# A two-layer decoder on one core: the large buffer moved to a multiple of 512 bytes, and expert blocks loaded plainly and turned on TensorE

## The reference, cut to what matters

```python
x = x + L0_attn(layernorm(x))          # windowed attention
x = x + L0_xattn(ctx, layernorm(x))    # 8 heads of 128 over 1536 keys (context and x)
x = x + L0_ffn(layernorm(x))           # ternary weights, depthwise convolution
x = x + L1_attn(layernorm(x))          # 16 heads of 16
x = x + L1_xattn(layernorm(x), ctx)
x = x + L1_ffn(layernorm(x))           # each token goes to one of 8 experts:
#   idx = argmax(softmax(x @ Wg + bg));  y = gelu(x @ W1[idx] + b1[idx]) @ W2[idx] + b2[idx]
```

## Time and profile before

| | us |
|---|---|
| median of 3 runs | 2080.79 (2079.79 to 2083.28) |
| the profiled execution | 2085.14 |
| its span, first to last instruction | 2083.3 |
| latent stages of the four batches, about | 60 to 285, 560 to 770, 1040 to 1260, 1530 to 1760 |
| first load of a new block leaves | 2025.98 |
| last scatter starts | 2078.86 |

### The profile page before, as it was taken

How to read it: one execution, slowest core, us unless ns; L and a number is a source line. 1 busy time by engine, 2 the same in 40 slices (tenths; PEclk the granted TensorE clock), 3 DMA queues, 4 the chain that set the end, 5 groups by cost and what they waited for, 6 DMA issues and landing times.

```text
span 2083.3 us, 41861 instructions
## 1 busy us (share of the span) xinstructions
PE 1849.1 (89%) x17118; PEld 1032.0 (50%) x17118; DVE 1634.8 (78%) x2654; ACT 1281.7 (62%) x1921; POOL 213.8 (10%) x223
## 2 busy tenths in 40 slices
PE   4999988989899987889899998898989998898967
PEld 2666653323566663232457665242356666333235
DVE  7888878697788877689688887969687887869944
ACT  5666646568566645749656664657756664574932
POOL 1000001110100001030100000120010000103513
PEclk8999999999999999999999999999999999999988
DMA  7477730000277760001157673001127666001125
GB/s 303 88 124 122 123 81 12 9 27 22 59 129 123 122 125 18 6 23 33 31 103 125 122 124 64 13 9 27 42 57 120 123 122 127 8 6 48 58 78 114
DMA packets 450766, 159.93 MB, mean 77 GB/s; under 512 B 426213, under 2 KB 441840, under 8 KB 450064
## 3 DMA queue, kind: packets, MB, share of 16 engines
q1 hardware_dynamic: 448192, 150.89, 35.9%
q0 software_dynamic: 2384, 6.36, 0.9%
HBM read 33.96 MB, written 9.47 MB: 21 GB/s over the span
## 4 chain that ended last, share of the span: by engine, by line
PE 49%; DVE 29%; DMA 9%; ACT 6%; issue 4%; SPq 1%; POOL 1%; POOLq 0%; DVEq 0%; ACTq 0%
DVE nmx L2234 15%; DMA arena<-arena 8%; PE ps L772 8%; PE ps L774 7%; PE ps L773 7%; PE ps L1154 6%; PE ps L944 3%; PE ps L1140 3%; DVE arena L2044 3%; PE ps L938 2%; PE ps L939 2%; PE ps L1104 1%; PE ps L1164 1%; DVE st L1866 1%; ACT arena L1542 1%
## 5 line engine op out<-in xcount | busy, mean ns | idle before, releaser
L2234 DVE TENSOR_REDUCE nmx<-ps 128x2 f32<-128x1024 f32 x384 | 444.4, 1217 | 14.0 <-PE ps L1104 12.5
L1714 ACT ACTIVATE arena<-ps 128x512 f32<-128x512 f32 x768 | 406.4, 600 | 47.8 <-PE ps L1140 43.4
L2029 DVE TENSOR_SCALAR_CACHE_REDUCE ps<-ps 128x1536 f32<-128x1536 f32 x128 | 225.7, 1763 | 44.2 <-PE ps L774 43.6
L1154 PE MATMUL ps<-arena 128*17 128x256 f32 x3072 | 240.0, 389 | 0.0
L2044 DVE SCALAR_TENSOR_TENSOR arena<-arena,rs 128x1536 f16<-128x1536 f32 x128 | 231.6, 1809 | 4.2 <-ACT arena L1604 4.2
L1604 ACT ACTIVATE arena<-arena,rs 128x1536 f16<-128x1536 f32 x128 | 200.8, 1569 | 42.9 <-DVE rs L2035 42.9
L1595 ACT ACTIVATE arena<-ps,nm 128x1536 f32<-128x1536 f32 x128 | 197.1, 1540 | 13.5 <-DVE ps L2029 13.5
L772 PE MATMUL ps<-arena 128*128 128x512 f16 (+2 forms) x508 | 176.4, 349 | 13.9 <-issue 7.0
L938 PE MATMUL ps<-arena 128*128 128x128 f16 x1536 | 185.3, 219 | 1.1 <-DMA arena<-arena 1.0
L939 PE MATMUL ps<-arena 128*128 128x128 f16 x1536 | 185.2, 219 | 0.0
L774 PE MATMUL ps<-arena 128*128 128x512 f16 (+2 forms) x508 | 176.2, 349 | 0.0
(11 more groups left out here) (350 smaller groups left out, 3562.5 us busy)
## 6 DMA issues: line engine op xcount, KB each, us to landing
arena<-in_weights SPq DMA_DIRECT2D x8, 929.0 KB, 21.1
arena<-arena SPq DMA_DIRECT2D x72, 64.0 KB, 2.1
arena<-arena SPq DMA_TRANSPOSE x268, 3.7
arena<-in_ctx SPq DMA_DIRECT2D x4, 1024.0 KB, 5.4
arena<-in_ctx_t SPq DMA_DIRECT2D x4, 1024.0 KB, 5.0
arena<-in_experts SPq DMA_DIRECT2D x1, 3840.0 KB, 11.7
arena<-zx_d SPq DMA_DIRECT2D x23, 132.0 KB, 2.2
arena<-arena SPq DMA_DIRECT2D x72, 32.0 KB, 1.9
```

Of the source, the lines that this page charges most:

```text
L1154: mm(ps[32 * j:32 * j + VW, 7, cols], v17[:, kt, 4 * g_ + j, :], pr_[:, (4 * t + j) % RING, cols], start=(kt + half == 0), stop=(kt == mod ...
L1714: A(pr_[:, n % RING, :], ps[:, 4 + n % 3, :], ACT.Exp).then_inc(b_exp.sem, 1)
L2029: TS_(s_, s_, -XS, None, ALU.mult, ALU.min, accum_out=nm[:, i:i + 1]).then_inc(s_max.sem, 1)
L2234: V.tensor_reduce(nmx[:, g_ % 2, ch, :, pp, i], ps[:, 2 * (z % 2):2 * (z % 2) + 2, :], AX.X, ALU.max, negate=True)\
```

## The change

1. `ident16` (256 bytes a partition) and `quant` (128 bytes) are allocated before `arena` instead of after it.
2. The reads of `rows_at` and `weights_at` lose their bounds checks. The new blocks' start rows are read one at a time, each just before its load, and the wait for the last scatter stands between the first read and the first load. TensorE reads two places, then one in each turn of the loop.
3. A block comes in one plain DMA of 128 x 2080 bytes into a ring of six buffers `block`; `xb` and `zr` are its two parts. It waits only for the scatter. TensorE turns the four 128 x 128 fp16 squares into PSUM (`turn_block`), ScalarE copies them to one of three `zb` (`turned`). The turn of block j+2 stands between hidden of j and out of j-1. Hidden of block 2 and the turns of blocks 2 and 3 come after the last routing, since they share its banks.
4. nc.Block's variable is now `blk`: a name alone.

```diff
+        ident16 = sb("ident16", [P, P], F16)
+        quant = sb("quant", [P, 2, 4, NT])
         ARENA = 96 * 1024 + 512
         arena = sb("arena", [P, ARENA // 4])
...
-        zb = [lay.take([4, P], F16) for _ in range(BR)]
-        xb = [lay.take([XW]) for _ in range(BR)]
+        block = [lay.take([ZW]) for _ in range(BR)]
+        xb = [t[:, D:ZW] for t in block]
+        zr = [t[:, 0:D].bitcast(F16) for t in block]
+        zb = [lay.take([4, P], F16) for _ in range(3)]
...
                 if j >= BR:
-                    sp.wait_ge(e_h.sem, e_h.at(0, 2 * (j - BR)) + 2)
                     sp.wait_ge(o_out[r_].sem, 16 * (j // BR))
-                rows = zx_d[bass.ds(at, P), :]
-                sp.dma_start_transpose(zb[r_], rows[:, 0:D].bitcast(F16)).then_inc(block_in[r_].sem, 16)
-                sp.dma_start(xb[r_], rows[:, D:ZW]).then_inc(block_in[r_].sem, 16)
+                sp.dma_start(block[r_], zx_d[bass.ds(at, P), :]).then_inc(block_in[r_].sem, 16)
...
             sp.wait_ge(e_table.sem, e_table.at(0, 4))
-            new = rows_at(OLD, NB)
-            sp.wait_ge(zx_out.sem, zx_out.at(B, 0))
             for j in range(OLD, NB):
-                load_block(j, new[j - OLD])
+                at = rows_at(j, j + 1)[0]
+                if j == OLD:
+                    sp.wait_ge(zx_out.sem, zx_out.at(B, 0))
+                load_block(j, at)
...
+            def turn_block(j):
+                r_ = j % BR
+                pe.wait_ge(block_in[r_].sem, block_in[r_].at(0, 16 * (j // BR + 1)))
+                if j >= 2:
+                    pe.wait_ge(e_zt.sem, e_zt.at(0, j - 1))
+                for k in range(4):
+                    last = nc.tensor.transpose(ps[:, LAST_BANK[j % 2], :].bitcast(F16)[:, P * k:P * k + P], zr[r_][:, P * k:P * k + P], ident16[:])
+                last.then_inc(e_t.sem, 1)
...
                 pe.wait_ge(e_table.sem, e_table.at(0, 4))
-                at += weights_at(OLD, NB)
+                at += weights_at(OLD, OLD + 2)
                 pe.wait_ge(e_table.sem, e_table.at(0, 6))
+                for j in range(OLD, OLD + 2):
+                    turn_block(j)
                 for j in range(OLD, NB + 1):
                     if j < NB:
                         block_hidden(j, at[j])
+                    if j + 2 < NB:
+                        turn_block(j + 2)
+                        at += weights_at(j + 2, j + 3)
                     block_out(j - 1, at[j - 1])
...
+                def turned(j):
+                    act.wait_ge(e_t.sem, e_t.at(0, j + 1))
+                    if j >= 3:
+                        act.wait_ge(e_h.sem, e_h.at(0, 2 * (j - 3)) + 2)
+                    A(zb[j % 3].rearrange("p a n -> p (a n)"), ps[:, LAST_BANK[j % 2], :].bitcast(F16)[:, 0:4 * P], ACT.Copy).then_inc(e_zt.sem, 1)
...
                 for j in range(OLD, NB):
                     gelus(j)
+                    if j + 2 < NB:
+                        turned(j + 2)
```

More of the change, by code:

```diff
@@ L150, in decoder @@
         ident = sb("ident", [P, P])
-        ident16 = sb("ident16", [P, P], F16)
         prefix = sb("prefix", [P, P + 2], F16)
@@ L164, in decoder @@
         c_rstd = sb("c_rstd", [P, NCTX // P])
-        quant = sb("quant", [P, 2, 4, NT])
         wsum = sb("wsum", [P, 2])
@@ L378, in decoder @@
         block_in = [w_in[k].again(16) for k in range(BR)]
+        e_t, e_zt = (w_in[k].again(16) for k in (6, 7))
         o_out = [sig(f"o_out{k}") for k in range(BR)]
@@ L468, in decoder @@
         assert [m.n_slots for m in MODES] == [39, 71]
-        block = c_.enter_context(nc.Block())
-        @block.sync
+        BOUNDED = "the table clamps the expert to the last one, and a block starts at most at its expert's count"
+        blk = c_.enter_context(nc.Block())
+        @blk.sync
         def _(sp):
@@ L619, in _ @@
             sp.wait_ge(e_table.sem, e_table.at(0, 4))
-            new = rows_at(OLD, NB)
-            sp.wait_ge(zx_out.sem, zx_out.at(B, 0))
             for j in range(OLD, NB):
-                load_block(j, new[j - OLD])
+                at = rows_at(j, j + 1)[0]
+                if j == OLD:
+                    sp.wait_ge(zx_out.sem, zx_out.at(B, 0))
+                load_block(j, at)
             for r_ in range(BR):
                 sp.wait_ge(o_out[r_].sem, 16 * len(range(r_, NB, BR)))
-        @block.gpsimd
+        @blk.gpsimd
         def _(pool):
@@ L761, in _ @@
                 scatter_block(j)
-        @block.tensor
+        @blk.tensor
         def _(pe):
@@ L1401, in weights_at @@
                 return nc.values_load_multi_w_load_instructions(where[0:1, 0, j0:j1], engines=(mybir.EngineType.PE,),
-                                                                min_val=0, max_val=2 * (NE - 1) * EW)[1]
+                                                                min_val=0, max_val=2 * (NE - 1) * EW,
+                                                                skip_runtime_bounds_check_because=BOUNDED)[1]
             def block_hidden(j, at):
-                r_ = j % BR
-                pe.wait_ge(block_in[r_].sem, block_in[r_].at(0, 32 * (j // BR + 1)))
+                pe.wait_ge(e_zt.sem, e_zt.at(0, j + 1))
                 for m in range(DC):
@@ L1412, in block_hidden @@
                                    [(tuple(ewc[:, HE * part + D * c + P * m:][:, bass.ds(at, P)] for part in range(2)),
-                                     (zb[r_][:, c, :], zb[r_][:, DC + c, :])) for c in range(DC)])
+                                     (zb[j % 3][:, c, :], zb[j % 3][:, DC + c, :])) for c in range(DC)])
                     last.then_inc(e_h.sem, 1)
+            def turn_block(j):
[6 more added lines that the diff above has]
+                last.then_inc(e_t.sem, 1)
             def block_out(j, at):
@@ L1438, in experts @@
                 for j in range(2):
+                    turn_block(j)
+                for j in range(2):
                     block_hidden(j, at[j])
+                pe.wait_ge(e_zt.sem, e_zt.at(0, 2))
                 transpose_last()
@@ L1443, in experts @@
                 route_logits(B - 1)
-                block_hidden(2, at[2])
                 route_ranks(B - 1)
-                for j in range(3, OLD):
+                pe.wait_ge(r_slots.sem, r_slots.at(B - 1, 1))
+                for j in range(2, 4):
+                    turn_block(j)
+                for j in range(2, OLD):
                     block_hidden(j, at[j])
-                    block_out(j - 1, at[j - 1])
+                    if j > 2:
+                        block_out(j - 1, at[j - 1])
+                    if j + 2 < OLD:
+                        turn_block(j + 2)
                 pe.wait_ge(e_table.sem, e_table.at(0, 4))
-                at += weights_at(OLD, NB)
+                at += weights_at(OLD, OLD + 2)
                 pe.wait_ge(e_table.sem, e_table.at(0, 6))
+                for j in range(OLD, OLD + 2):
+                    turn_block(j)
                 for j in range(OLD, NB + 1):
@@ L1474, in _ @@
             experts()
-        @block.scalar
+        @blk.scalar
         def _(act):
@@ L1812, in experts @@
             def experts():
+                def turned(j):
[3 more added lines that the diff above has]
+                    A(zb[j % 3].rearrange("p a n -> p (a n)"), ps[:, LAST_BANK[j % 2], :].bitcast(F16)[:, 0:4 * P], ACT.Copy).then_inc(e_zt.sem, 1)
                 load_table(3, ACT.Gelu)
                 act.wait_ge(e_table.sem, e_table.at(0, 3))
+                for j in range(2):
+                    turned(j)
                 for j in range(2):
@@ L1835, in _ @@
             experts()
-        @block.vector
+        @blk.vector
         def _(dve):
```

5 lines of the change are left out of this document (3 added, 2 removed).

## The result

The changed kernel takes 2055.03 us (median of 4 runs, 2051.15 to 2055.69), the kernel before 2082.03 on the same chip (2079.79 to 2083.58): ratio 0.9867, 95% interval 0.985 to 0.9884. Forecast were 2070 and a gain of 11 us; it gained 27. The profiled execution took 2055.47 us with a span of 2053.7, so the spans can be compared: 29.6 us less than 2083.3.

The account below looks back on a forecast made before the run. TensorE was taken to bound the latent stages, waiting for DMA transposes, and SyncE, the ring and TensorE by turns the tail. -13.5 (place) + 2.5 (tail) = -11 us gave 2070 us at the median, range 2061 to 2083.

Parts of the forecast that it names:

- Part 1: Latent stages: the arena's new place makes each softmax-weight transpose land 0.4 us sooner, -13.5 us in all.
- a third: DMA transposes: of the 11.8 ns extra cost per 256-byte packet, 4 ns taken as due to the place.
- the 36 waits: TensorE's waits at L944 for the DMA transposes of the softmax weights, 30.0 us in all; each to shrink by up to 0.4.
- The upper bound of -23: Part 1's largest gain, about -23 us, if the place saves 1.13 us a transpose.
- Part 2: Start of the tail: single unchecked address reads (0.43 us SyncE, 0.50 TensorE) gain 5.3 us, bounds 4 and 6.
- H(5): The 12 hidden products (L772 to L774) of block 5, the first new block; forecast to start at 2025.7 instead of 2031.04.
- Part 3: Tail: plain loads and TensorE turns make the buffer ring bind at 2.87 us a block; tail +2.5, bounds -5 and +11.
- sign of TensorE waiting at the turn in nearly each block: Tail: block pitch 2.9 us, with TensorE waiting at the new transpose for arena<-zx_d in nearly each block.
- The place costs nothing: Rival, chance 0.20: alignment gains nothing in the transposes, only the tail's +2.5 or more remains; about 2084 us.
- The place costs most of it: Rival, chance 0.08: alignment saves 0.8 to 1.1 us a transpose, -20 to -23 us; 2062 or below with the tail.
- the ring doesn't bind: Rival, chance 0.12: quick scatters or a hidden read on TensorE let the tail keep its 5 us; 2062 us.
- Low clock: Rival, chance 0.05: waits keep TensorE at its low clock in the tail, about +4 us; 2074 us.

Follow-up runs that it names:

- the kernel with the arena at 256: The kernel before with only quant (128 bytes) ahead of the arena, which then starts on an odd multiple of 256: 2055.4 us, ratio 0.9861.
- The two runs with one source off: The changed kernel with only the hi transposes' sources (L509) 128 bytes off: 2058.98 us; with only the lo ones' (L526): 2086.06 us.
- the two runs of the place alone: The kernel before with ident16 and quant ahead of the arena: 2055.5 us; the changed kernel with the old allocation order: 2088.56 us.

## Why the prediction was right or wrong

**Part 1, the step that failed: what a shorter landing is worth.** The place acts as described, though through the source alone, and its size per packet was close: 3.5 ns less (21.6 to 18.1) where 4 was taken, 0.5 us of landing where 0.4 was. That closeness is luck, since no row stood behind "a third". What fell short was "a wait shrinks by the smaller of itself and 0.4. The typical one vanishes, a 2 us one loses 0.4. 36 x 0.4 = 14.4 us, less about 1". I set TensorE's starts of both traces against each other at each of the 36 waits, against the kernel with the arena at 256 and against the changed one:

| | forecast | measured |
|---|---|---|
| 25 waits listed under 1 us | 10 | 13.2 |
| 5 long waits that vanish (1.8 to 2.3 each) | 2 | 10.6 |
| 6 long waits that stay (0.1 to 0.8 less each) | 2.4 | 2.0 to 4.3 |
| elsewhere up to the end of the last latent stage | 0 | 2.7 to 4.1 |
| sum | 13.5 (after 1 off) | 28.5 to 32.1 |

- *Five of the eleven long waits vanish whole.* 8.6 us of the error. Each stood behind a lo transpose that was slow, 5.3 to 5.6 us, and an instruction fetch (queue q8, 16 KB a packet) fell into its flight. The one issued at 176.24 (below its source line and landing, then for 176.24 to 181.78 the GB/s in 40 slices and the queue's row) had its pieces through by 180.1 except for a few, which came at 7 to 11 GB/s from 180.8 to 181.5, behind the fetch that started at 179.87:

```profile
L522 SPq DMA_TRANSPOSE arena<-arena x1: 1423/1423/1423, 176.2 to 176.2; - x1
...
DMA to landing us min/median/max: 5.5/5.5/5.5
```

```profile
GB/s 0 0 0 0 0 0 0 0 54 213 226 213 214 216 207 205 220 214 216 174 163 165 217 244 213 174 272 22 52 0 0 0 0 9 7 9 11 9 105 286
...
q8 instruction: 1, 0.02, 1.1%
```

  After, the same transpose was issued at 174.37 and landed at 177.6; the next fetch came at 177.25, after its last piece. So what vanished was not 0.4 us but the meeting: the five land in 3.2 to 3.3 us in all eleven traces with the lo source on a multiple of 256, and in 5.3 to 5.6 in all five with it off. Three other long waits stood behind transposes that are slow in every trace (4.0 to 5.7 us); they stay, and the 3.4 us wait at 1736.38 only shrinks to 2.6. The last three stood behind transposes of the usual 3.8 us.

  Meetings as such are not gone. Of the transposes that took over 3 us in the trace before, 81 had a fetch under way between 1.5 us behind their issue and their landing, and of these 38 took more than 4.3 us, of the 181 others 4. After it is 27 of 64 and 1 of 194. No experiment moved the fetches, so that the fetch is what holds a transpose up is read from the traces and not tested.
- *Short waits were read too small.* The listed idle of 0.40 counts from the modelled end of the matmul before, which overlaps the pitch. In starts it is 207.41 - 206.80 = 0.61 where it is 0.05 after (202.64, 202.69). The matmul before the wait, in the old timeline:

```profile
206.80 0.22 PE L939 MATMUL ps<-arena 128*128 128x128 f16 x1
```

  And the lo transpose of such a head landed 0.6 us sooner, not 0.4: in 3.8 us before (issued at 203.54) and 3.2 after (199.38). The two runs with one source off show that lo is the one that counts. The 1.3 us that a landing 0.45 us shorter, in place of 0.4, was to add are some 0.75 by the forecast's own rule, since only waits over 0.4 gain from it.
- *What moved outside the 36 waits* (2.7 to 4.1 us) was put at nothing; I have not traced it to a cause.
- The upper bound of -23 was made from the same idle times and so excluded what happened.

**Part 2** was right in kind and too small: H(5) 6.3 us earlier where 5.3 was forecast, just outside the bounds of 4 and 6, the reads 0.28 and 0.30 us where 0.43 and 0.50 were.

**Part 3** was right in its mechanism: the ring is the bound, 2.94 a block over all 17 where 2.87 was forecast, load 2.8 and scatter 2.4 where 2.45 and 2.5 were taken. Its sign of TensorE waiting at the turn in nearly each block did not come: 8 turns waited, and on the chain a scatter and a load take 1.3 us more together than their medians, in each of four rounds, where I had allowed 3 us in all. From the first gelu of H(5) to the end the new loop takes 60.2 us and the old one 51.3 (2083.3 - 2031.97), 8.9 more against 7.8 forecast. With part 2 that is +2.6 against +2.5: two small errors that cancel.

**The rivals.** "The place costs nothing" is refuted by the two runs of the place alone. "The place costs most of it" and "the ring doesn't bind" came nearest in their time (both 2062), neither by its mechanism: a transpose gained 0.5 us and not 0.8 to 1.1, and the ring binds. "Low clock" is seen in parts of the tail (0.81) but goes with the ring's waits.

## What to carry to other kernels

Put SBUF buffers that DMA transposes read from on a multiple of 256 bytes; it costs an allocation's order and gave 1.3% here, and the side written to was free. When a loop is late by a little in every round, price a shorter link by the pitch of starts, not by the listed idle. Look up which transfer stands behind each long wait: one that is slow because it meets something else can lose far more than the shortening, or nothing. Before trading a DMA's work for an engine's, count the iterations that a buffer passes through from use to use: two more buffers turned a loss of 9 us into a draw.

## What the runs showed of the hardware

- A source 32 or 128 bytes off a multiple of 256 slows a DMA transpose of 1536 packets of 256 bytes from 3.2 to 3.7 us from issue to landing, and its issue on SyncE from 1.41 to 1.43; a destination 128 off changes next to nothing (3.23 us against 3.20 for the same transposes).
- A register read of one value took 0.28 us on SyncE and 0.30 on TensorE's sequencer, less than a line through the reads of 5 and 18 values says (0.43 and 0.50). The Trainium skill (DMA: Bandwidth & Descriptors, Latency and other measured facts) gives some 600 ns as the floor of such a load; these rows are under it.
- Instruction fetches, 16 KB a packet, run on the 16 DMA engines beside the kernel's own transfers. Five transposes with one in flight took 5.3 to 5.6 us where 3.7 is usual; a correlation, not tested.
